# A fused transformer layer and expert feed-forward: attention in steps of two head pairs, value projections of 512 columns

## The chip, the cores and the metric

The kernel runs on one core of a Trainium2 chip. Its engines are TensorE (PE, matmuls; its weight loads are shown as PEld), VectorE (DVE), ScalarE (ACT), GpSimd (POOL) and SyncE (SP, which issues the DMAs). The metric is the device time of one execution in microseconds; the median of the runs counts, and lower is better. Of the kernel before there are 3 timed runs.

## The reference

All in float32, for x of 8 x 256 x 256 (batch, tokens, features):

```python
def attention(x, ctx, mask, wq, wk, wv, wo, bo):        # 16 heads of 64
    q, k, v = (heads of x @ wq), (heads of ctx @ wk), (heads of ctx @ wv)
    sim = einsum('bhid,bhjd->bhij', q, k) * 64 ** -0.5
    sim = where(mask[:, None, None, :], neg, sim)
    out = einsum('bhij,bhjd->bhid', softmax(sim), v)
    return out as (b, n, 1024) @ wo + bo

h = layernorm(x)                                        # no gain, no bias
h = layernorm(h + attention(h, h, mask, sa_...), ln1)
h = layernorm(h + attention(h, ctx_1024, mask, ca_...), ln2)
h = layernorm(h + gelu(h @ fc1_w + fc1_b) @ fc2_w + fc2_b, ln3)
x = x + h
xf = layernorm(x)
y = geglu(xf, w1s, w2s, w3s) + geglu(xf, W1[e], W2[e], W3[e])   # e = argmax(xf @ Wg) of 8
return x + y
```

## The kernel before

The instructions of each engine are written out by hand, one list per engine, and the engines meet through counting semaphores. The program has three parts: the attention (self layer, then cross layer, up to some 770 us), a dense stage of 8 steps (fc1, fc2) and a stage of expert steps. The change touches the first part and the passage to the second.

Every float32 product is made of three fast ones (`product`, L49 to L54): each operand is split into a high part (`_hi`, rounded by a copy) and a low part (`_lo`, what is left), and low x high, high x low and high x high are summed in PSUM. So each tensor that PE multiplies costs a copy on ACT (or DVE) and a subtraction on DVE (or POOL).

A **turn** u is one batch element in one layer: 16 turns, 0 to 7 of the self layer, 8 to 15 of the cross layer. A turn has 8 **pairs** of heads; pairs i are counted through, 128 in all (`NPAIR`). For a pair:
- `project_qk(i)`: q and k of both heads into one bank `ps_pj`; ACT copies it (`hi_of_bank`), DVE subtracts (`lo_of_bank`, L1515).
- `scores(i)` (L960): 12 matmuls of 64 rows, two heads side by side, into `ps_s[0]` and `ps_s[1]`. They wait for qk's low part (`pj_lo`) and for the masked maxima of the pair before (`max_ready`).
- `masked_max(i, h)` (L1533): DVE adds the mask, writes `scores` to SBUF and takes the row extreme `nb`.
- `exps(i, h)` (L1294): ACT, `probs` and their sums; `invert_sums` (L1543, DVE); `normalise` (L669, POOL).
- `transpose_probs(i, h)` (L970): 4 PE transposes per head into `ps_t[h]`; ACT copies (`hi_of_probs`, L1301), DVE subtracts (`lo_of_probs`, L1547).
- `attend(i)` (L983): 8 matmuls into `ps_pv`, of which there is one; high and low part of the values stand side by side, so that the product comes in two halves. ACT copies the lower half (`cross_of_pair`, L1305), DVE adds it to the upper (`join_pair`, L1555, two adds), ACT and POOL split the result (`hi_of_pair` L1310, `lo_of_pair` L688). The next `attend` waits for the join.
- `output(i)`: 6 matmuls into `ps_aux`, two pairs at a time.

Besides, every second pair `project_v(g)` makes the values of the next two pairs (group g, 12 matmuls of 256 columns; L1282, L1513), and once per turn the next turn's rows are transposed (`xq`), in the cross layer its context too (`xc`; L1519). DVE adds the residual once per turn (L1563) and takes row statistics: of the output of the turn before (`output_stats`) and, in the self layer, of the next input (`input_stats`; L1568, L1571). POOL norms rows (L674 to L678), applies gain and bias (L701, L702) and the attention's bias (L710). The weights of a layer come in as 512-column pieces: DVE copies the high part (L1499), POOL subtracts (L719), at pairs given by `PIECES_IN`.

The order around the change is one loop over i on each engine. In iteration i PE issues scores(i+1), transposes of i, project_qk(i+2), on even i output of two pairs, on some the values or rows, attend(i-1). DVE does the maxima of i+1, join of i-2, then the low parts, and after them rows, weight pieces and statistics. The names of the banks are shared out by `bank_events`, which lists everything that goes through the two `ps_pj` in order.

Of the kernel before, what the change touches and what calls it, by code (L numbers as in the profile page):

```python
# [75 lines left out]

def bank_events():

    order = [("xq", 0), ("qk", 0), ("qk", 1), ("v", 0)]
    for i in range(NPAIR):  # L80
        u, p = i // PAIRS, i % PAIRS
        if i + 2 < NPAIR:
            order.append(("qk", i + 2))
        if p == CTX_AT and u + 1 < NTURN and layer_of(u + 1):
            order.append(("xc", u + 1))
        if p == ROWS_AT and u + 1 < NTURN:
            order.append(("xq", u + 1))
        if p % 2 == 1 and i + 1 < NPAIR:
            order.append(("v", (i + 1) // 2))
        if i == FIRST_ROWS_AT:  # L90
# [1787 lines left out]
```

## Time and profile before

| | us |
|---|---|
| runs: median (lowest to highest) | 1227.9 (1227.55 to 1228.11) |
| the profiled execution | 1228.37 |
| its span, first to last instruction | 1226.6 |
| PE busy in it | 1211.9 |
| DVE busy | 981.8 |
| ACT busy | 874.9 |
| POOL busy | 681.2 |

The span is what the trace covers; the execution's own time has 1.8 us around it. Busy time counts the work of an engine, not its waits. A matmul's record shows how long it takes from start to end, 0.28 us, though the next starts 0.12 us later; what matmuls cost is therefore read from start to start. The same holds for ACT and DVE, whose instructions overlap a little.

### The profile page before, as it was taken

Reading aid. Unit: us, or ns where it says so; the run is one execution under the profiler, and the core shown is the slowest. Engines: PE = TensorE matmul, PEld = TensorE weight load, DVE = VectorE, ACT = ScalarE, POOL = GpSimd, SP = SyncE. Lnnn points to the kernel's source line nnn. Section 1 sums busy time; section 2 is a strip of 40 time slices with the busy share of each in tenths; the row PEclk is TensorE's granted clock in tenths of the full one; section 3 lists DMA queues with packets and bytes.
Section 4 is the critical chain, followed back from the end, with each engine's and each line's share of the span. In section 5 each row is a group of like instructions: output and inputs, shape, how many; then the busy total and the mean of one; then the engine's idle time right before and its main releaser. Section 6 shows DMA issues by size and latency. Waiting matters only on the chain.

```text
span 1226.6 us, 31369 instructions
## 1 busy us (share of the span) xinstructions
PE 1211.9 (99%) x10444; PEld 1163.3 (95%) x10444; DVE 981.8 (80%) x2674; ACT 874.9 (71%) x2259; POOL 681.2 (56%) x1089
## 2 busy tenths in 40 slices
PE   8999999999999999999999999999999999999998
PEld 6899999999999999999999999999999999999998
DVE  6888888988989988888888889854554888888854
ACT  6988888878887888888888788543433677767732
POOL 5766656656678855555565477887624033432231
PEclk9999999999999999999999999999999999999999
DMA  6060000000000002200000010111013677788722
GB/s 198 4 248 19 18 3 19 10 11 19 7 22 27 2 27 110 91 27 28 2 28 28 2 36 12 35 41 47 1 64 122 190 262 252 251 257 277 236 69 78
DMA packets 72207, 97.46 MB, mean 79 GB/s; under 512 B 5488, under 2 KB 52464, under 8 KB 72048
## 3 DMA queue, kind: packets, MB, share of 16 engines
q1 hardware_dynamic: 70512, 91.25, 22.9%
q0 software_dynamic: 1536, 4.20, 1.1%
q8 instruction: 86, 1.41, 0.5%
q14 instruction: 73, 0.60, 0.2%
HBM read 81.01 MB, written 14.42 MB: 78 GB/s over the span
## 4 chain that ended last, share of the span: by engine, by line
PE 84%; DVE 6%; ACT 5%; issue 3%; DMA 1%; SPq 0%; DVEq 0%; ACTq 0%
PE ps_pj L52 9%; PE ps_pj L54 9%; PE ps_pj L53 9%; PE ps_t L970 8%; PE ps_s L960 8%; PE ps_pv L983 8%; PE ps_aux L54 4%; PE ps_aux L52 4%; PE ps_aux L53 4%; ACT probs L1294 4%; PE ps_s L54 4%; PE ps_s L53 4%; PE ps_s L52 4%; PE ps_pv L54 2%; PE ps_pv L52 2%
## 5 line engine op out<-in xcount | busy, mean ns | idle before, releaser
L669 POOL TENSOR_SCALAR probs<-probs,inv 128x256 f32<-128x256 f32 x512 | 235.7, 479 | 220.9 <-DVE inv L1543 220.2
L1294 ACT ACTIVATE probs<-scores,nb 128x256 f32<-128x256 f32 x512 | 253.7, 497 | 16.5 <-DVE nb L1533 16.0
L1533 DVE CUSTOM_DVE_ANT_0 scores<-ps_s,maskf 128x256 f32<-128x256 f32 x512 | 186.7, 420 | 54.1 <-PE ps_s L960 51.7
L1301 ACT ACTIVATE probs_t_hi<-ps_t 128x512 fp32r<-128x512 f32 x256 | 150.7, 589 | 99.7 <-PE ps_t L970 99.6
L1547 DVE TENSOR_TENSOR probs_t_lo<-ps_t,probs_t_hi 128x512 fp32r<-128x512 f32 x256 | 172.8, 675 | 0.4
L970 PE MATMUL ps_t<-ident,probs 128*128 128x128 f32 x1024 | 139.9, 279 | 0.6 <-POOL probs L669 0.6
L52 PE MATMUL ps_pj<-xq_hi,wq_lo 128*128 128x256 f32 x448 | 138.1, 308 | 0.1
L983 PE MATMUL ps_pv<-probs_t_lo,v_stack 128*128 128x256 f32 x512 | 130.3, 287 | 1.1 <-issue 1.0
L983 PE MATMUL ps_pv<-probs_t_hi,v_stack 128*128 128x256 f32 x512 | 127.7, 282 | 0.0
L970 PEld LDWEIGHTS ps_t<-ident,probs 128*128 128x128 f32 x1024 | 109.7, 141 | 17.8 <-POOL probs L669 0.9
L54 PE MATMUL ps_pj<-xq_hi,wq_hi 128*128 128x256 f32 x448 | 126.2, 282 | 0.0
L53 PE MATMUL ps_pj<-xq_lo,wq_hi 128*128 128x256 f32 x448 | 126.2, 282 | 0.0
L688 POOL TENSOR_TENSOR heads_t_lo<-joined,heads_t_hi 128x256 fp32r<-128x256 f32 x128 | 94.6, 739 | 31.1 <-ACT heads_t_hi L1310 30.7
L1555 DVE TENSOR_TENSOR joined<-ps_pv,cross 64x256 f32<-64x256 f32 x256 | 106.1, 415 | 3.0 <-ACT cross L1305 1.2
L1515 DVE TENSOR_TENSOR qk_lo<-ps_pj,qk_hi 128x512 fp32r<-128x512 f32 x128 | 88.5, 691 | 14.1 <-ACT qk_hi L1285 2.9
L983 PEld LDWEIGHTS ps_pv<-probs_t_lo,v_stack 128*128 128x128 f32 x512 | 97.9, 191 | 1.7 <-issue 1.7
L816 POOL TENSOR_TENSOR wq_lo<-raw,wq_hi 128x512 fp32r<-128x512 f32 x14 | 18.1, 1294 | 145.7 <-ACT wq_hi L1408 145.7
L983 PEld LDWEIGHTS ps_pv<-probs_t_hi,v_stack 128*128 128x128 f32 x512 | 98.0, 191 | 0.0
L1385 ACT ACTIVATE gelu<-ps_pj 128x512 f32<-128x512 f32 x78 | 46.5, 596 | 72.2 <-PE ps_pj L54 71.0
L1294 ACT ACTIVATION_READ_ACCUMULATOR probs<-scores,nb 128x1 f32 x512 | 95.6, 187 | 0.0
L1394 ACT ACTIVATE gt_hi<-ps_s 128x512 fp32r<-128x512 f32 x64 | 38.3, 599 | 75.7 <-DVE ps_s L1603 75.7
L960 PE MATMUL ps_s<-qk_hi,qk_lo 64*128 64x256 f32 x512 | 85.5, 331 | 6.7 <-DVE qk_lo L1515 6.0
(275 smaller groups left out, 4439.5 us busy)
## 6 DMA issues: line engine op xcount, KB each, us to landing
raw<-in_L_ffn_W SPq DMA_DIRECT2D x90, 512.0 KB, 4.9
slot_rows<-hin SPq DMA_DIRECT2D x3, 768.0 KB, 6.1
rows<-in_x SPq DMA_DIRECT2D x8, 256.0 KB, 2.7
after_self<-rows SPq DMA_DIRECT2D x8, 256.0 KB, 2.1
rows<-after_self SPq DMA_DIRECT2D x8, 256.0 KB, 2.7
cin<-in_ctx SPq DMA_DIRECT2D x8, 256.0 KB, 3.0
after_cross<-rows SPq DMA_DIRECT2D x8, 256.0 KB, 2.7
stage<-in_L_xattn_fc_w SPq DMA_DIRECT2D x2, 1024.0 KB, 9.0
```

The source lines that it names most:

```text
L52: pe.matmul(out, wl, mh, start=start, stop=False, skip_group_check=True)
L53: pe.matmul(out, wh, ml, start=False, stop=False, skip_group_check=True)
L54: return pe.matmul(out, wh, mh, start=False, stop=stop, skip_group_check=True)
L669: last = pool.tensor_scalar(PR[:, h, t, :], PR[:, h, t, :], inv[:, h, t:t + 1], 1.0, ALU.mult, ALU.mult)
L960: last = pe.matmul(ps_s[h][:, t * S:(t + 1) * S], q[a][half, t * P:(t + 1) * P], k[b][half, :], start=t == 0 and n == 0, stop=t == ST - 1 ...
L970: last = pe.transpose(ps_t[h][:, j * S + t * P:j * S + (t + 1) * P], PR[:, h, t, j * P:(j + 1) * P], ident[:, :])
L983: last = pe.matmul(ps_pv[:, h * S:(h + 1) * S], v, x[:, i % 2, h, j, :], start=h == 0 and j == 0 and x is PT[1], stop=j == ST - 1 and x is ...
L1294: last = act.activation(PR[:, h, t, :], SM[:, h, t, :], ACT.Exp, bias=nb[:, h, t:t + 1], scale=-1.0, accum_out=sums[:, h, t:t + 1])
L1301: act.activation(flat(PT[0][:, i % 2, h, :, :]), ps_t[h][:, :], ACT.Copy).then_inc(t_hi, 1)
L1533: last = dve.tensor_tensor_reduce(SM[:, h, t, :], ps_s[h][:, t * S:(t + 1) * S], maskf[:, i // PAIRS % 2, :], -SCALE, -LOWEST, ALU.add, AL ...
L1547: dve.tensor_tensor(flat(PT[1][:, i % 2, h, :, :]), ps_t[h][:, :], flat(PT[0][:, i % 2, h, :, :]).bitcast(F32), ALU.subtract).then_inc(t_l ...
L1555: last = dve.tensor_tensor(joined[h * DH:(h + 1) * DH, i % 2, :], ps_pv[0:DH, h * S:(h + 1) * S], cross[:, h, :], ALU.add)
```

## The change

The attention runs in **steps of two pairs**: step k works on i = 2k, 63 steps (`TURNS_OF_TWO`), four to a turn.
- PE in step k: scores of pairs i+2 and i+3, project_qk(i+4), attend(i), values, transposes of i+1 and i+2, project_qk(i+5), output of two pairs, rows or context, attend(i+1).
- Scores of even pairs go to `ps_s`, of odd pairs to `ps_t`, and the transposes of a pair go to the other two banks (`scores_bank`, `turned_bank`). Scores now wait for the low parts of the probabilities transposed through that bank (`t_lo`), transposes for the maxima that empty theirs.
- The masked maxima write into `probs` itself, of which there are now three, and `nb`, `sums`, `inv` are doubled.
- DVE starts a step with the join of pair i-1, ahead of the maxima of i+2 and i+3.
- From turn 1 on, a value group is one of the two 128-row tiles of the keys for four pairs (`project_v`: 6 matmuls of 512 columns in place of 12 of 256), and `VS` is two blocks of four pairs.
- Weight pieces, statistics, norms and rows are put to steps in place of pairs. The load of the shared w3 waits for the last attend. Two of the dense stage's first products change places with banks.

```diff
+AHEAD = [("v", 1), ("q", 2), ("k", 2), ("q", 3)]
+STARTS = (0, 26, 58)
+PIECES_IN = [{0: [("k", 3), ("v", 2), ("o", 0)], 1: [("v", 3), ("o", 1)], 2: [("o", 2)], 3: [("o", 3)]},
+             {0: [("q", 0), ("k", 0)], 1: [("q", 1), ("v", 0)], 2: [("k", 1), ("v", 1), ("q", 2)], 3: [("k", 2), ("v", 2)],
+              4: [("v", 3), ("q", 3)], 5: [("k", 3), ("o", 0)], 6: [("o", 1)], 7: [("o", 2)], 8: [("o", 3)]},
+             {0: [("q", 0), ("k", 0)], 1: [("v", 0), ("q", 1)], 2: [("k", 1), ("q", 2)], 3: [("v", 1), ("q", 3)],
+              4: [("o", 0)], 5: [("o", 1)], 6: [("o", 2)], 7: [("o", 3)], 8: [("k", 2), ("v", 2), ("k", 3), ("v", 3)]}]
...
             def project_v(g):
...
+                else:
+                    t, half = g % 2, k // 2
                     for c in range(KC):
+                        last = product(pe, bank[:, :], tuple(x[:, c, t * P:(t + 1) * P] for x in kv_of(u)),
+                                       tuple(w[:, c * INNER + half * 512:c * INNER + (half + 1) * 512] for w in W["v"]),
+                                       c == 0, c == KC - 1)
...
             def scores(i):
                 pe.wait_ge(pj_lo, EVENT[("qk", i)] + 1)
-                wait(pe, max_ready, 2 * i)
+                if i == 2:
+                    pe.wait_ge(max_ready, 2)
+                elif i > 2:
+                    pe.wait_ge(t_lo, 2 * (i - 2))
...
             def transpose_probs(i, h):
                 pe.wait_ge(norm_ready, 2 * i + h + 1)
-                wait(pe, t_lo, 2 * (i - 1) + h + 1)
+                if i == NPAIR - 1:
+                    pe.wait_ge(t_lo, 2 * (i - 2) + h + 1)
+                else:
+                    pe.wait_ge(max_ready, 2 * (i + 1) + h + 1)
```

PE's list (in part; the old loop over i is taken out):

```diff
+            for k in range(TURNS_OF_TWO):
+                i = 2 * k
+                scores(i + 2)
+                scores(i + 3)
+                if i + 4 < NPAIR:
+                    project_qk(i + 4)
+                attend(i)
+                for g in values_in(k):
+                    project_v(g)
...
+                for n in (i + 1, i + 2):
+                    transpose_probs(n, 0)
+                    transpose_probs(n, 1)
+                if i + 5 < NPAIR:
+                    project_qk(i + 5)
+                if k >= 1:
+                    output(i - 2)
+                    output(i - 1)
+                if turn_rows(k) is not None:
+                    what, u = turn_rows(k)
+                    (transpose_ctx if what == "xc" else transpose_rows)(u)
+                attend(i + 1)
```

ACT's list of a step:

```diff
+                if k >= 1:
+                    cross_of_pair(i - 1)
+                exps(i + 2, 0)
+                exps(i + 2, 1)
+                if i + 4 < NPAIR:
+                    hi_of_bank(("qk", i + 4))
+                if k >= 1:
+                    hi_of_pair(i - 1)
+                cross_of_pair(i)
+                exps(i + 3, 0)
+                for g in values_in(k):
+                    hi_of_bank(("v", g))
...
+                hi_of_probs(i + 1, 0)
+                hi_of_probs(i + 1, 1)
+                hi_of_pair(i)
+                hi_of_probs(i + 2, 0)
+                hi_of_probs(i + 2, 1)
+                exps(i + 3, 1)
+                if i + 5 < NPAIR:
+                    hi_of_bank(("qk", i + 5))
+                if turn_rows(k) is not None:
+                    hi_of_bank(turn_rows(k))
```

DVE's list of a step:

```diff
+                if k >= 1:
+                    join_pair(i - 1)
+                masked_max(i + 2, 0)
+                masked_max(i + 2, 1)
+                invert_sums(i + 2, 0)
+                masked_max(i + 3, 0)
+                invert_sums(i + 2, 1)
+                masked_max(i + 3, 1)
+                if i + 4 < NPAIR:
+                    lo_of_bank(("qk", i + 4))
+                join_pair(i)
+                invert_sums(i + 3, 0)
+                if p == 1 and u >= 1:
+                    residual_sum(u - 1)
+                for g in values_in(k):
+                    lo_of_bank(("v", g))
...
+                lo_of_probs(i + 1, 0)
+                lo_of_probs(i + 1, 1)
+                lo_of_probs(i + 2, 0)
+                lo_of_probs(i + 2, 1)
+                invert_sums(i + 3, 1)
+                if i + 5 < NPAIR:
+                    lo_of_bank(("qk", i + 5))
+                if turn_rows(k) is not None:
+                    lo_of_bank(turn_rows(k))
+                if k < TURNS_OF_TWO - 1:
+                    late_hi_pieces(k)
...
+                if p == 1 and u >= 1:
                     output_stats(u - 1)
-                if p == 1 and u + 1 < B:
+                if p == 0 and u + 1 < B:
                     input_stats(u + 1)
```

The built programs show the order that results. On ACT, in the cross layer, two pairs before (L1301 copies transposed probabilities, L1294 is the exponentials, L1285 qk, L1282 values, L1310 a joined pair, L1305 the crossing half):

```order
L1294 ACTIVATE probs,sums<-scores,nb 128x256 x4
L1285 ACTIVATE qk_hi<-ps_pj 128x512
L1301 ACTIVATE probs_t_hi<-ps_t 128x512
L1310 ACTIVATE heads_t_hi<-joined 128x256
L1305 ACTIVATE cross<-ps_pv 64x512
L1301 ACTIVATE probs_t_hi<-ps_t 128x512
L1294 ACTIVATE probs,sums<-scores,nb 128x256 x4
L1285 ACTIVATE qk_hi<-ps_pj 128x512
L1301 ACTIVATE probs_t_hi<-ps_t 128x512
L1282 ACTIVATE v_stack<-ps_pj 128x8x64
L1310 ACTIVATE heads_t_hi<-joined 128x256
L1305 ACTIVATE cross<-ps_pv 64x512
```

and one step of two pairs in the change (L1359, L1352, L1342, L1339, L1368, L1363 in the same meaning):

```order
L1363 ACTIVATE cross<-ps_pv 64x512
L1352 ACTIVATE probs_68,sums<-probs_68,nb 128x256 x4
L1342 ACTIVATE qk_hi<-ps_pj 128x512
L1368 ACTIVATE heads_t_hi<-joined 128x256
L1363 ACTIVATE cross<-ps_pv 64x512
L1352 ACTIVATE probs_69,sums<-probs_69,nb 128x256 x2
L1339 ACTIVATE v_stack_61<-ps_pj 128x8x64
L1359 ACTIVATE probs_t_hi<-ps_s 128x512 x2
L1368 ACTIVATE heads_t_hi<-joined 128x256
L1359 ACTIVATE probs_t_hi<-ps_t 128x512 x2
L1352 ACTIVATE probs_69,sums<-probs_69,nb 128x256 x2
L1342 ACTIVATE qk_hi<-ps_pj 128x512
```

The exponentials of four heads now stand in three places (two heads, one, one), the first of them right behind a crossing copy, and the copy of the second qk is last in the step.

On DVE, one pair before, from its last masked maximum (L1533) to the next pair's first (L1555 join, L1543 inverted sums, L1547 and L1515 low parts of probabilities and qk):

```order
L1533 ISA scores,nb<-ps_s,maskf 128x256
L1533 ISA nb 128x1
L1555 TENSOR_TENSOR joined<-ps_pv,cross 64x256 x2
L1543 RECIPROCAL inv<-sums 128x2
L1547 TENSOR_TENSOR probs_t_lo<-ps_t,probs_t_hi 128x512
L1543 RECIPROCAL inv<-sums 128x2
L1515 TENSOR_TENSOR qk_lo<-ps_pj,qk_hi 128x512
L1547 TENSOR_TENSOR probs_t_lo<-ps_t,probs_t_hi 128x512
L1533 ISA scores,nb<-ps_s,maskf 128x256
```

and the second half of a step in the change, up to the next step's first maximum (L1589, L1633, L1621, L1587, L1625, L1610 in the same meaning; L1593 is the low part of the context):

```order
L1589 TENSOR_TENSOR qk_lo<-ps_pj,qk_hi 128x512
L1633 TENSOR_TENSOR joined<-ps_pv,cross 64x256 x2
L1621 RECIPROCAL inv<-sums 128x2
L1587 TENSOR_TENSOR v_stack_61<-ps_pj,v_stack_61 128x8x64
L1625 TENSOR_TENSOR probs_t_lo<-ps_s,probs_t_hi 128x512 x2
L1625 TENSOR_TENSOR probs_t_lo<-ps_t,probs_t_hi 128x512 x2
L1621 RECIPROCAL inv<-sums 128x2
L1589 TENSOR_TENSOR qk_lo<-ps_pj,qk_hi 128x512
L1593 TENSOR_TENSOR xc_lo<-ps_pj,xc_hi 128x512
L1633 TENSOR_TENSOR joined<-ps_pv,cross 64x256 x2
L1610 ISA probs_69,nb<-ps_s,maskf 128x256
```

The join has moved from behind the maxima to ahead of them, and the low parts of the second qk and of the context, which stood behind the probabilities' low parts, now stand just ahead of that join.

On PE, the switch from scores (L960) to transposes (L970) to projections before:

```order
L960 MATMUL ps_s<-qk_lo,qk_hi 128x256 x2
L960 MATMUL ps_s<-qk_hi 128x256 x2
L970 MATMUL ps_t<-ident,probs 128x128 x8
L52 MATMUL ps_pj<-xq_hi,wq_lo 128x256
L53 MATMUL ps_pj<-xq_lo,wq_hi 128x256
```

and scores to projections (L999 is the scores) in the change:

```order
L999 MATMUL ps_s<-qk_lo,qk_hi 128x256 x2
L999 MATMUL ps_s<-qk_hi 128x256 x2
L999 MATMUL ps_t<-qk_hi,qk_lo 128x256 x2
L999 MATMUL ps_t<-qk_lo,qk_hi 128x256 x2
L999 MATMUL ps_t<-qk_hi 128x256 x2
L999 MATMUL ps_t<-qk_hi,qk_lo 128x256 x2
L999 MATMUL ps_t<-qk_lo,qk_hi 128x256 x2
L999 MATMUL ps_t<-qk_hi 128x256 x2
L52 MATMUL ps_pj<-xq_hi,wq_lo 128x256
L53 MATMUL ps_pj<-xq_lo,wq_hi 128x256
L54 MATMUL ps_pj<-xq_hi,wq_hi 128x256
```

Scores of an even pair and an odd pair stand together, and projections follow them.

## Rows read from the trace of the kernel before

**Rows 1.** The page, span and part 1: busy time and share of the span.

```profile
span 1226.6 us, 31369 instructions
...
PE 1211.9 (99%) x10444; PEld 1163.3 (95%) x10444; DVE 981.8 (80%) x2674; ACT 874.9 (71%) x2259; POOL 681.2 (56%) x1089
```

**Rows 2.** Windows view, one self turn: us; busy PE, PEld, DVE, ACT, POOL; clock; DMA.

```profile
302.78:349.43 46.65, 46.55 (x422) 44.33 (x420) 40.76 (x135) 38.06 (x109) 29.03 (x55) 1.00 0.06 19
```

**Rows 3.** Timeline, PE, one pair: start, us, what (x how many).

```profile
650.28 0.28 PE L983 MATMUL ps_pv<-probs_t_hi,v_stack 128*128 128x256 f32 x1
...
650.72 0.28 PE L960 MATMUL ps_s<-qk_lo,qk_hi 64*128 64x256 f32 x2
...
651.19 0.28 PE L960 MATMUL ps_s<-qk_hi 64*128 64x256 f32 x2
651.40 1.09 PE L970 MATMUL ps_t<-ident,probs 128*128 128x128 f32 x8
...
652.45 0.28 PE L53 MATMUL ps_pj<-xq_lo,wq_hi 128*128 128x256 f32 x1
```

**Rows 4.** Timeline, PE, start-up, where projections follow scores.

```profile
16.72 0.31 PE L960 MATMUL ps_s<-qk_hi 64*128 64x256 f32 x2
...
17.18 0.28 PE L53 MATMUL ps_pj<-xq_lo,wq_hi 128*128 128x256 f32 x1
...
18.49 1.04 PE L970 MATMUL ps_t<-ident,probs 128*128 128x128 f32 x8
...
19.49 0.28 PE L53 MATMUL ps_pj<-xq_lo,wq_hi 128*128 128x256 f32 x1
```

**Rows 5.** Timeline, PE, 512 moving columns, in the routed stage.

```profile
980.22 0.40 PE L53 MATMUL ps_pj<-wk_lo,xq_hi 128*128 128x512 f32 x1
980.45 0.39 PE L54 MATMUL ps_pj<-wk_hi,xq_hi 128*128 128x512 f32 x1
```

**Rows 6.** Timeline, ACT, one pair.

```profile
646.83 0.50 ACT L1294 ACTIVATE probs<-scores,nb 128x256 f32<-128x256 f32 x1
...
648.81 0.57 ACT L1285 ACTIVATE qk_hi<-ps_pj 128x512 fp32r<-128x512 f32 x1
649.28 0.58 ACT L1301 ACTIVATE probs_t_hi<-ps_t 128x512 fp32r<-128x512 f32 x1
...
650.24 0.41 ACT L1310 ACTIVATE heads_t_hi<-joined 128x256 fp32r<-128x256 f32 x1
650.67 0.60 ACT L1305 ACTIVATE cross<-ps_pv 64x512 f32<-64x512 f32 x1
```

**Rows 7.** Timeline, DVE, the same pair.

```profile
647.04 0.42 DVE L1533 CUSTOM_DVE_ANT_0 scores<-ps_s,maskf 128x256 f32<-128x256 f32 x1
...
647.39 0.85 DVE L1555 TENSOR_TENSOR joined<-ps_pv,cross 64x256 f32<-64x256 f32 x2
...
649.41 0.69 DVE L1515 TENSOR_TENSOR qk_lo<-ps_pj,qk_hi 128x512 fp32r<-128x512 f32 x1
650.02 0.68 DVE L1547 TENSOR_TENSOR probs_t_lo<-ps_t,probs_t_hi 128x512 fp32r<-128x512 f32 x1
...
651.22 0.74 DVE L1568 BATCH_NORM_STATS2 part<-rows 128x6 f32<-128x256 f32 x2
...
652.27 0.42 DVE L1533 CUSTOM_DVE_ANT_0 scores<-ps_s,maskf 128x256 f32<-128x256 f32 x1
```

**Rows 8.** Timeline, PE, scores of pairs 10, 50, 74 and 122.

```profile
68.78 0.39 PE L960 MATMUL ps_s<-qk_hi,qk_lo 64*128 64x256 f32 x2
...
302.87 0.39 PE L960 MATMUL ps_s<-qk_hi,qk_lo 64*128 64x256 f32 x2
...
445.17 0.39 PE L960 MATMUL ps_s<-qk_hi,qk_lo 64*128 64x256 f32 x2
...
726.61 0.39 PE L960 MATMUL ps_s<-qk_hi,qk_lo 64*128 64x256 f32 x2
```

**Rows 9.** Line view, L1499: 128x512 copies of weight pieces, min/median/max ns.

```profile
L1499 DVE CAST wk_hi<-stage x8: 412/475/1503, 356.0 to 779.6; 128x512 fp32r<-128x512 f32 x8
```

More of the change, by code:

```diff
@@ L74, in layer_of, with turn_rows @@
     return u // B
-def bank_events():
[L79 to L90, printed above, removed]
+def turn_rows(k):
+    u = k // STEPS_PER_TURN + 1
+    if u < NTURN and k % STEPS_PER_TURN == 0 and layer_of(u):
+        return ("xc", u)
+    if u < NTURN and k % STEPS_PER_TURN == 1:
+        return ("xq", u)
+    return None
@@ L91, in bank_events, with values_in @@
+def values_in(k):
+    if k < 3:
+        return ((1,), (2,), (3, 4))[k]
+    return (k + 2,) if 2 * k + 4 < NPAIR else ()
+def bank_events():
+    order = [("xq", 0), ("qk", 0), ("qk", 1), ("v", 0), ("qk", 2), ("qk", 3)]
+    for k in range(TURNS_OF_TWO):
+        if 2 * k + 4 < NPAIR:
+            order.append(("qk", 2 * k + 4))
+        order += [("v", g) for g in values_in(k)]
+        if k == TURNS_OF_TWO - 1:
             order.append(("h", 0))
+        if 2 * k + 5 < NPAIR:
+            order.append(("qk", 2 * k + 5))
+        if turn_rows(k) is not None:
+            order.append(turn_rows(k))
@@ L128, in set_of @@
+PIECES_AT = {start + at: pieces for start, plan in zip(STARTS, PIECES_IN) for at, pieces in plan.items()}
 def set_of(i):
-    return sum(i >= base for base in BASES[1:])
+    return sum(i >= start for start in STARTS[1:])
 LATE = [(0, kind, q) for kind, q in AHEAD] + [(set_of(j), kind, q) for j in sorted(PIECES_AT) for kind, q in PIECES_AT[j]]
@@ L863, in _ @@
+            split_late(TURNS_OF_TWO - 1)
             lo_of_pair(NPAIR - 2)
-            split_late(NPAIR)
+            split_late(TURNS_OF_TWO)
             lo_of_pair(NPAIR - 1)
-            for i in range(NPAIR + 1, NPAIR + 4):
-                split_late(i)
+            split_late(TURNS_OF_TWO + 1)
+            split_late(TURNS_OF_TWO + 2)
             bias_rows(0)
@@ new lines, in _ @@
+            scores(1)
+            project_qk(2)
+            transpose_probs(0, 0)
+            transpose_probs(0, 1)
+            project_qk(3)
+            for k in range(TURNS_OF_TWO):
+                i = 2 * k
+                scores(i + 2)
[5 more added lines that the diff above has]
+                    project_v(g)
+                if k == TURNS_OF_TWO - 1:
+                    transpose_first(0)
+                for n in (i + 1, i + 2):
[10 more added lines that the diff above has]
+                attend(i + 1)
@@ L1215, in _ @@
+            up_dense(0, 0)
+            attend(NPAIR - 2)
+            up_dense(0, 1)
+            transpose_probs(NPAIR - 1, 0)
+            transpose_probs(NPAIR - 1, 1)
+            output(NPAIR - 4)
+            output(NPAIR - 3)
+            attend(NPAIR - 1)
+            transpose_step(1)
+            up_dense(0, 2)
+            up_dense(0, 3)
+            output(NPAIR - 2)
+            output(NPAIR - 1)
             down(0, range(FC))
@@ L1280, in hi_of_bank @@
                 if kind == "v":
-                    wait(act, pv_done, 2 * (k - 1))
-                    last = act.activation(v_part(k, 0), v_rows(bank), ACT.Copy)
+                    wait(act, pv_done, 4 * (k // 2 - 1))
+                    last = act.activation(v_part(k, 0), v_rows(bank, k), ACT.Copy)
                 elif kind == "qk":
```

316 lines of the change are left out of this document (146 added, 170 removed), and 6 rows, old and new, of the table PIECES_IN.

## The prediction

> **What bounds the kernel now.** I read first the page's part 1: TensorE (PE) is busy 1211.9 of 1226.6 us, VectorE (DVE) 80%, ScalarE (ACT) 71% [rows 1]. Then one turn of the attention, 46.65 us long: PE 46.55 busy, DVE 40.76, ACT 38.06, POOL 29.03, clock 1.00 [rows 2]. So PE sets the pace, and DVE has 5.9 us of slack in a turn of eight pairs. The change touches the attention alone; the rest is read as fixed. The reader is to see two more things. A turn of the self layer takes (302.87 - 68.78)/5 = 46.8 us, the three turns in which the second layer's weight pieces come in take 142.3 together, and the six up to pair 122 take 281.4, 46.9 each [rows 8]. And PE's own stream has gaps that are no waits: matmuls of 256 columns follow each other every 0.12 us, but where the 64-row scores begin two intervals take 0.44 in place of 0.24 (+0.20), from scores to transposes 0.21 (+0.09), and from the first transpose to the second projection matmul behind the eight it is 1.05 [rows 3], against 1.00 where no scores stood just before (+0.05) [rows 4].
>
> **The change on PE.** For two pairs the old order pays 2 x (0.20 + 0.09 + 0.05) = 0.68 us of these switches. The new one issues the scores of two pairs together, puts projections behind them, and transposes both pairs together behind other matmuls. That is one entry (0.20) and one way out to projections, which the start-up shows as 0.46 for 0.24 (+0.22) [rows 4], and nothing ahead of the transposes. Scores of one pair straight behind those of another occur nowhere in the trace: between 0 and 0.20; I take 0, for within a pair the scores follow each other without a gap. So 0.42, a saving of 0.26 in each of 63 steps, 16.4 us. Value projections: from turn 1 on a group is 6 matmuls of 512 columns in place of 12 of 256, in 60 groups, 360 fewer. 512 columns take 0.23 [rows 5] against 2 x 0.12, so 12 x 0.12 - 6 x 0.23 = 0.06 less a group, 3.6 us in all. PE alone would then need 20.0 us less. A pair takes it (46.55 - 0.44)/8 = 5.76 us now (the turn's four transposes of rows taken off at 0.11), so a step of two pairs 11.52 - 0.26 - 0.06 = 11.20 us.
>
> The Trainium skill (TensorE: Matmul & The Clock Gate, Back-to-back issue gap) gives N/2.4 + 2.5 ns for a gap, 109 and 216 ns: by the page a group would gain 12 x 109 - 6 x 216 = 12 ns, 0.7 us in all. The rows show 120 and 230, and decide.
>
> **The change on DVE and ACT.** Their work stays the same, but the new order ties them into a loop. I walk through one step k, i = 2k, from the start of the join of pair i-1 (J), with start-to-start times of [rows 6, 7]:
> - DVE: the join is two adds, 0.85; head 0 of pair i+2 then takes two masked maxima at 0.35 and 0.07 until the last one ends. With a hand-over of 0.03 (ACT's copy of qk ends at 648.81 + 0.57 = 649.38, its low part starts at 649.41) ACT starts its exponentials at J + 1.65. Until then ACT had only the crossing copy of pair i-1 to do, which the join itself needed.
> - ACT from there has an unbroken list up to the copy of qk(i+5): four heads' exponentials at 0.99 (646.83 to 648.81 is two heads), 3.96; qk(i+4) 0.47; values 0.48; four copies of transposed probabilities 1.92; two of joined pairs 0.86; one crossing copy, between 0.43 (as the joined pair's) and 0.60 (its duration), I take 0.50, what other copies of 512 columns take; the copy of qk(i+5) 0.57 and hand-over 0.03. Sum 8.79, so J + 10.44. PE is not waited for in it: PE's scores begin 0.74 before J, and 1.6 of scores, 1.6 of projection, 1.0, 1.4 of values and 1.7 of transposes end at J + 6.6; the copies of the last two heads start at 7.9 and 8.4.
> - DVE then takes the low part of qk(i+5), 0.61: J + 11.05. Behind it stands the join of pair i+1.
>
> So the loop takes 11.05 us, just under PE's 11.20. That is the bare step. Whatever DVE does between that low part and the next join is added whole, since ACT has nothing meanwhile: the low part of the next turn's rows or context 0.60; statistics 1.05 (651.22 to 652.27) [rows 7]; a weight piece some 0.45 (0.475 [rows 9] less a little overlap). Before, these stood in DVE's slack ahead of the maxima, where ACT had transposed probabilities to copy. The residual sum (0.6, an add of 128x512) stays free: DVE idles about as long at the wait for the last exponentials behind it.
>
> Can PE hide the excess? Little. Its next step needs qk(i+5) split for its second scores, which leaves some 0.15 us of room; past that PE stands. POOL is busy 29.0 us in a turn [rows 2], 7.3 per step; it is off this loop except where a step bunches its work (a rival, below). SP: context, rows and weights are still issued a step or more ahead. The one load moved behind the last attention is w3s, needed a dense step later: no cost; if late, its copies on ACT would hold the second dense step.
>
> **The sum.** A self turn: 4 x 11.05 + 0.60 rows + 1.05 input + 1.05 output statistics + 0.1 (PE's 11.20 in the step where the lag is gone) = 47.0. A cross turn: 44.2 + 1.2 + 1.05 + 0.1 = 46.55.
> - Turn 0: two copies of first weight pieces (0.48 each) enter ACT's list in step 0: +1.0.
> - Turns 1 to 5: 5 x 47.0 = 235.0 against 234.1: +0.9.
> - Turns 6 to 8: 47.0 + 4 pieces (1.8); turn 7, without input statistics, 44.2 + 1.2 + 1.05 + 9 pieces (4.05) = 50.5; turn 8 46.55 + 3 pieces (1.35). Together 147.2 against 142.3: +4.9.
> - Turns 9 to 14: 6 x 46.55 + 4 pieces = 281.1 against 281.4: -0.3.
> - Last turn and the passage to the dense stage: both orders wait there; between -4 and +2, I take -1.
>
> That is +5.5 us. The profiled execution took 1228.4 (its span 1226.6), 0.5 above the median of the runs, 1227.9. So 1233.9 for an execution like the profiled one, 1233.4 as the median.
>
> **Rivals.**
> - *PE stays the bound*: the loop is cut somewhere (extras fall into DVE's idle time, ACT starts before the join is done). Then switches and projections count in full: 1227.9 - 20.0 = 1207.9. For it: PE is 99% busy, nothing else is near it. Against: DVE would need 40.8 of 45.2 us and never be waited for. Chance 0.14. The Trainium skill (Perfetto Trace Analysis, Identifying the Most-Contended Engine) says to optimize the engine of the highest occupancy first; by that rule PE's savings pay and this rival wins. The walk above is where I part from it.
> - *The loop is shorter by 0.15 a step* (join and maxima overlap more, a cheaper crossing copy): 0.15 x 63 = 9.5 less, 1224. Chance 0.20.
> - *Slower still, through POOL*: in a turn's third step POOL norms the output rows between the pairs it normalises. It decides once that step's work passes 11.2, 4 us above its mean of 7.3, and normalised probabilities come later than PE's transposes want them. At 0.6 us in each of 14 turns, 8.4: 1242. Chance 0.11.
> - *The change does not do what it says*: the built order shows 360 fewer matmul rows and the moves quoted above. No chance given.
>
> **Numbers.** Forecast 0.55, by itself 1227 to 1240 (0.1 us a step is 6 us in all). A difference under 0.2%, 2.5 us, is what a measurement of this kernel can't tell from none. Faster by more: 0.14 of PE's bound, 0.11 of the shorter loop: 0.25. Same: 0.09 of the shorter loop, 0.07 of the forecast: 0.16. Slower: 0.59. The range, 1214 to 1243, leaves out PE's bound and a little above.
>
> **What would show it.** Right: PE waits for qk_lo (L1589) at the scores of odd pairs, most in the steps behind statistics; ACT's largest wait is at the exponentials, for DVE's nb, 1.0 us or more a step; turns of 47.0 and 46.6; PE busy falls by some 20 us while the span grows; no gap from scores to scores; values every 0.23. Wrong: turns of 45.2 to 45.7 with PE above 98%; a bare step well off 11.1; ACT waiting mostly for PE's transposes, as before; statistics that do not lengthen their step.

## The result, and the profile of the changed kernel

The changed kernel takes 1257.79 us (median of 4 runs, 1255.87 to 1259.34) against 1228.01 (4 runs, 1227.55 to 1228.42): a ratio of 1.024, 95% interval 1.0227 to 1.0253. I had said 1233.4, 1214 to 1243. The sign was right, the size was not: 5.5 us more were forecast and 29.8 came. The profiled execution took 1258.6 us, its span is 1256.9, 30.3 above the span of before [rows 1].

The page of the changed kernel, with the chain of waits (its part 4):

```profile
span 1256.9 us, 30952 instructions
...
PE 1221.2 (97%) x10084; PEld 1150.6 (92%) x10084; DVE 983.4 (78%) x2674; ACT 879.0 (70%) x2259; POOL 685.6 (55%) x1089
...
PE 59%; DVE 14%; ACT 14%; issue 9%; POOL 1%; DVEq 1%; DMA 1%; SPq 0%; ACTq 0%; POOLq 0%
```

The work of DVE, ACT and POOL is what it was, but DVE and ACT now hold 28% of the chain. Before, it was 11%:

```profile
PE 84%; DVE 6%; ACT 5%; issue 3%; DMA 1%; SPq 0%; DVEq 0%; ACTq 0%
```

The waits over the whole span (engine, tile and line, what it waited for; us, times, longest) name the place:

```profile
ACT probs L1352 <- DVE nb L1610: 145.1, 65, 4.2
...
DVE inv L1621 <- ACT probs L1352: 64.3, 114, 1.1
...
PEld ps_t L999 <- DVE qk_lo L1589: 17.9, 33, 1.7
```

ACT stands 2.2 us in each step until DVE's first maxima are there, and PE's scores of odd pairs wait for the low part of qk: the two signs that the prediction named. The windows view (us; busy PE, PEld, DVE, ACT, POOL; clock; DMA) of the four steps of a self turn, cut at the attention products of pairs 40, 42, 44, 46 and 48:

```profile
271.24:282.57 11.33, 11.33 (x101) 10.66 (x100) 9.66 (x32) 8.63 (x25) 6.80 (x12) 1.00 0.01 2
282.57:294.75 12.18, 12.18 (x104) 11.14 (x103) 10.83 (x34) 9.95 (x28) 7.28 (x15) 1.00 0.00 0
294.75:307.53 12.78, 11.92 (x100) 10.65 (x99) 10.74 (x39) 10.34 (x30) 9.47 (x17) 1.00 0.01 3
307.53:318.82 11.29, 11.29 (x101) 10.66 (x99) 9.51 (x31) 9.44 (x28) 5.54 (x11) 1.00 0.15 48
```

The same four steps took 11.68, 11.95, 11.50 and 11.51 before, 46.64 in all, and take 47.58 now. The two bare steps are shorter than before, by 0.35 and 0.22; the two behind statistics are longer, by 0.23 and 1.28.

One bare step of the loop, from the join of pair 43 to that of pair 45, in ACT's and DVE's timelines (start, us). DVE first:

```profile
293.71 0.81 DVE L1633 TENSOR_TENSOR joined<-ps_pv,cross 64x256 f32<-64x256 f32 x2
294.56 0.42 DVE L1610 CUSTOM_DVE_ANT_0 probs<-ps_s,maskf 128x256 f32<-128x256 f32 x1
...
304.35 0.69 DVE L1589 TENSOR_TENSOR qk_lo<-ps_pj,qk_hi 128x512 fp32r<-128x512 f32 x1
304.96 0.84 DVE L1633 TENSOR_TENSOR joined<-ps_pv,cross 64x256 f32<-64x256 f32 x2
```

```profile
295.37 0.51 ACT L1352 ACTIVATE probs<-probs,nb 128x256 f32<-128x256 f32 x1 [2.73 <-DVE nb L1610]
...
297.26 0.19 ACT L1352 ACTIVATION_READ_ACCUMULATOR probs<-probs,nb 128x1 f32 x1
297.48 0.60 ACT L1342 ACTIVATE qk_hi<-ps_pj 128x512 fp32r<-128x512 f32 x1
...
298.90 0.50 ACT L1352 ACTIVATE probs<-probs,nb 128x256 f32<-128x256 f32 x1
...
300.00 0.60 ACT L1339 ACTIVATE v_stack<-ps_pj 128x512 fp32r<-128x512 f32 x1
...
303.60 0.23 ACT L1352 ACTIVATION_READ_ACCUMULATOR probs<-probs,nb 128x1 f32 x1
303.69 0.62 ACT L1342 ACTIVATE qk_hi<-ps_pj 128x512 fp32r<-128x512 f32 x1
```

So the loop is there, link by link: join to first exponential 295.37 - 293.71 = 1.66 (forecast 1.65); ACT's list 304.35 - 295.37 = 8.98 (8.79); low part 0.61 (0.61); together 11.25 where I had 11.05.

**Places that the prediction did not walk.** In the third step of turn 0 (group 4 shares its bank with qk of pair 8) and in the last step, PE stands over 2 us. Its timeline at the two:

```profile
54.32 0.28 PE L54 MATMUL ps_pj<-wv_hi,xq_hi 128*128 128x256 f32 x1
56.96 0.77 PE L52 MATMUL ps_pj<-wv_hi,xq_lo 128*128 128x512 f32 x1 [2.36 <-DVE qk_lo L1589]
...
793.69 0.28 PE L54 MATMUL ps_aux<-wo_hi,heads_t_hi 128*128 128x256 f32 x1
796.15 0.39 PE L52 MATMUL ps_aux<-wo_hi,heads_t_lo 128*128 128x256 f32 x1 [2.17 <-POOL heads_t_lo L697]
```

and the windows around them, where the last but two columns are the granted clock:

```profile
54.00:56.00 2.00, 0.60 (x6) 0.40 (x4) 1.59 (x9) 1.95 (x7) 1.54 (x4) 1.00 0.00 0
56.00:58.00 2.00, 1.04 (x3) 0.88 (x4) 1.76 (x7) 1.90 (x6) 1.16 (x3) 0.67 0.01 4
58.00:60.00 2.00, 2.00 (x7) 1.51 (x6) 0.65 (x1) 0.10 (x1) 0.79 (x2) 0.50 0.00 0
...
794.00:796.00 2.00, 0.00 (x0) 0.00 (x0) 0.78 (x2) 0.25 (x1) 1.92 (x3) 1.00 0.00 0
796.00:798.00 2.00, 1.85 (x13) 1.85 (x14) 0.43 (x1) 0.00 (x0) 2.00 (x3) 0.84 0.71 217
798.00:800.00 2.00, 2.00 (x11) 2.00 (x11) 0.80 (x2) 1.41 (x3) 1.47 (x2) 0.50 0.68 196
```

Around the end of each wait the clock falls from 2.4 to 1.2 GHz for some 3 us, and the 512-column matmuls of group 4 follow each other every 0.43 us.

A third place lies in the last turn: PE's attention product waits 1.53 us for a join that stands on DVE behind two weight pieces and the statistics, and here too the clock falls (rows of DVE and PE, then the window).

```profile
777.07 0.54 DVE L1573 CAST wv_hi<-stage 128x512 fp32r<-128x512 f32 x1
777.87 0.74 DVE L1646 BATCH_NORM_STATS2 part<-rows 128x6 f32<-128x256 f32 x2
778.80 0.81 DVE L1633 TENSOR_TENSOR joined<-ps_pv,cross 64x256 f32<-64x256 f32 x2
779.72 0.36 PE L1025 MATMUL ps_pv<-probs_t_lo,v_stack 128*128 128x256 f32 x1 [1.53 <-issue]
...
780.00:782.00 2.00, 2.00 (x13) 2.00 (x12) 1.28 (x9) 1.54 (x7) 0.00 (x0) 0.58 0.00 0
```

With the one at 26 us (last section) the profiled execution has four such stretches of some 3.4 us, and the kernel before has none in its attention. An estimate from these windows: at half the clock they cost at most 4 x 1.7 = 6.8 us of the 30.3.

Where the 30.3 us of span went, by the starts of the attention products, beside what I had forecast for each stretch (for the first, no term at all):

| stretch | before | after | more | forecast |
|---|---|---|---|---|
| start to attention product 0 | 25.7 | 27.9 | 2.1 | 0 |
| turn 0 | 47.8 | 52.3 | 4.5 | 1.0 |
| turns 1 to 5 | 234.1 | 238.7 | 4.6 | 0.9 |
| turns 6 to 8 | 142.3 | 151.1 | 8.8 | 4.9 |
| turns 9 to 14 | 281.4 | 285.6 | 4.2 | -0.3 |
| last turn and all behind it | 495.3 | 501.3 | 6.0 | -1 |

### The profile page after: what moved, and what is told of

It is laid out like the page before. It is cut to its first block, busy times and chain, and to the rows that moved or that the text cites. A ratio compares the mean times of both kernels' runs of the same rounds, so it can differ in the third digit from the quotient of the medians.

```text
span 1256.9 us, 30952 instructions
## 1 busy us (share of the span) xinstructions
PE 1221.2 (97%) x10084; PEld 1150.6 (92%) x10084; DVE 983.4 (78%) x2674; ACT 879.0 (70%) x2259; POOL 685.6 (55%) x1089
## 4 chain that ended last, share of the span: by engine, by line
PE 59%; DVE 14%; ACT 14%; issue 9%; POOL 1%; DVEq 1%; DMA 1%; SPq 0%; ACTq 0%; POOLq 0%
PE ps_pj L52 7%; PE ps_pj L53 6%; PE ps_pj L54 6%; ACT probs_t_hi L1359 6%; ACT probs L1352 5%; DVE probs L1610 5%; PE ps_pv L1025 4%; PE ps_s L52 4%; PE ps_s L54 4%; PE ps_s L53 4%; DVE qk_lo L1589 3%; PE ps_aux L52 3%; PE ps_aux L54 3%; PE ps_aux L53 3%; PE ps_t L999 2%
## 5 line engine op out<-in xcount | busy, mean ns | idle before, releaser
L678 POOL TENSOR_SCALAR probs<-probs,inv 128x256 f32<-128x256 f32 x512 | 242.0, 485 | 261.6 <-DVE inv L1621 260.0
L1352 ACT ACTIVATE probs<-probs,nb 128x256 f32<-128x256 f32 x512 | 256.2, 507 | 145.1 <-DVE nb L1610 145.1
L1610 DVE CUSTOM_DVE_ANT_0 probs<-ps_t,maskf 128x256 f32<-128x256 f32 x256 | 98.4, 422 | 24.3 <-issue 15.8
L1633 DVE TENSOR_TENSOR joined<-ps_pv,cross 64x256 f32<-64x256 f32 x256 | 105.1, 411 | 7.3 <-ACT cross L1363 5.5
L1352 ACT ACTIVATION_READ_ACCUMULATOR probs<-probs,nb 128x1 f32 x512 | 101.0, 197 | 0.0
L52 PEld LDWEIGHTS ps_pj<-xq_hi,wq_lo 128*128 128x128 f32 x448 | 85.1, 190 | 13.0 <-DVE qk_lo L1589 0.9
L1459 ACT ACTIVATE gelu<-ps_pj 128x512 f32<-128x512 f32 x78 | 46.4, 595 | 72.2 <-PE ps_pj L54 70.9
L1621 DVE RECIPROCAL inv<-sums 128x2 f32<-128x2 f32 x256 | 42.1, 164 | 68.0 <-ACT probs L1352 64.3
L1589 DVE TENSOR_TENSOR qk_lo<-ps_pj,qk_hi 128x512 fp32r<-128x512 f32 x128 | 88.1, 688 | 8.7 <-ACT qk_hi L1342 3.0
L1610 DVE CUSTOM_DVE_ANT_0 probs<-ps_s,maskf 128x256 f32<-128x256 f32 x256 | 93.3, 421 | 1.9
L53 PEld LDWEIGHTS ps_pj<-xq_lo,wq_hi 128*128 128x128 f32 x448 | 85.6, 191 | 0.0
L54 PEld LDWEIGHTS ps_pj<-xq_hi,wq_hi 128*128 128x128 f32 x448 | 85.5, 191 | 0.0
```

The costliest lines, as they stand in the source:

```text
L52: pe.matmul(out, wl, mh, start=start, stop=False, skip_group_check=True)
L53: pe.matmul(out, wh, ml, start=False, stop=False, skip_group_check=True)
L54: return pe.matmul(out, wh, mh, start=False, stop=stop, skip_group_check=True)
L678: last = pool.tensor_scalar(x, x, inv[:, i % 2, h, t:t + 1], 1.0, ALU.mult, ALU.mult)
L1352: last = act.activation(x, x, ACT.Exp, bias=nb[:, i % 2, h, t:t + 1], scale=-1.0, accum_out=sums[:, i % 2, h, t:t + 1])
L1459: act.activation(G[:, f % 2, :], ps_u[f % 2][:, :], ACT.Gelu).then_inc(g_ready, 1)
```

## Experiments

Runs 1 to 4, 5 to 8 and 9 to 12 were timed in three sets, each beside the kernel before, whose medians were 1228.1, 1227.9 and 1228.4 us. A median is of 4 executions where nothing else is said.

**1. The join behind the maxima.** One part of the change undone:

```diff
-                if k >= 1:
-                    join_pair(i - 1)
                 masked_max(i + 2, 0)
                 masked_max(i + 2, 1)
+                if k >= 1:
+                    join_pair(i - 1)
```

> VectorE takes the two masked maxima pairs of pair i+2 ahead of the join of pair i-1; nothing else moves. Theory 1 (a loop through VectorE and ScalarE sets the step; the join of 0.85 us stands in it ahead of the maxima): the exponentials start some 0.75 us earlier in each step, the bare step of 11.28 us falls to what PE needs (11.20) and the steps with extras lose the whole 0.75. Self turn 47.6 -> 45.3 to 46.1, total 1224 to 1236, 1230 expected. Theory 2 (PE's own waits for the second bank of transposes and the late second scores set the step, the join is beside it): within 2 us of 1257.8. Theory 3 (the join is then late for the next attention product, PE waits for it instead): above 1257.8.

Measured: 1257.41 us (1256.09 to 1258.07), as the changed kernel. DVE's and PE's timelines show why:

```profile
292.99 0.84 DVE L1633 TENSOR_TENSOR joined<-ps_pv,cross 64x256 f32<-64x256 f32 x2
```

```profile
293.09 0.28 PE L54 MATMUL ps_pj<-xq_hi,wk_hi 128*128 128x256 f32 x1
293.94 0.35 PE L1025 MATMUL ps_pv<-probs_t_lo,v_stack 128*128 128x256 f32 x1 [0.57 <-issue]
```

PE's attention product of pair i writes the bank that the join of pair i-1 reads; with the join behind the maxima of both heads it stands until 293.83, and PE waits 0.57 us here and in every step (3.9 us in eight steps). Bare steps are 11.80, 0.5 longer than in the changed kernel. The number is the one of theory 2, "within 2 us of 1257.8", but it is a sum: turns 9 to 14 take 290.9 us against 285.6, while turn 0 takes 50.1 against 52.3 and the last stretch 497.8 against 501.3. Theory 3's wait is in the trace and outweighs theory 1's gain in the bare step. This run alone can't tell whether the loop was cut; run 6 does.

**2. Statistics moved** from the end of a step to behind the first two maxima of the next.

```diff
                 masked_max(i + 2, 1)
+                if p == 2 and u >= 1:
+                    output_stats(u - 1)
+                if p == 1 and u + 1 < B:
+                    input_stats(u + 1)
                 invert_sums(i + 2, 0)
...
-                if p == 1 and u >= 1:
-                    output_stats(u - 1)
-                if p == 0 and u + 1 < B:
-                    input_stats(u + 1)
```

> The statistics of input and output rows (1.05 us each, 7 + 15 of them inside the steps) move from behind the low part of qk(i+5) to behind the first masked maxima of the next step, where VectorE stands idle for 0.7 us. Theory 1 (work behind the low part of qk(i+5) is added whole to its step, work behind the maxima is not): 22 x 1.05 = 23 us less, 1235 (1232 to 1240), self turn 45.5. Theory 2 (the step is long for another reason, statistics only fill the wait): 1257 to 1259.

Measured: 1237.54 us (1236.87 to 1238.32), 20.3 less than the changed kernel, 0.92 for each of the 22 passes, in the range of theory 1. No work was taken away. The same four steps:

```profile
261.83:273.15 11.32, 11.32 (x101) 10.66 (x100) 9.70 (x32) 9.49 (x28) 6.80 (x12) 1.00 0.01 2
273.15:284.75 11.60, 11.60 (x104) 11.02 (x103) 11.14 (x38) 9.69 (x29) 7.28 (x15) 1.00 0.00 0
284.75:296.32 11.57, 11.44 (x101) 10.66 (x99) 10.40 (x37) 9.75 (x28) 9.48 (x17) 1.00 0.01 3
296.32:307.63 11.31, 11.31 (x101) 10.66 (x100) 9.50 (x31) 9.47 (x28) 5.54 (x11) 1.00 0.16 48
```

The steps with statistics fell from 12.18 and 12.78 to 11.60 and 11.57; the bare ones stay. What stands between the low part of qk(i+5) and the next maxima is added to the step, as the prediction had it.

**3. Values of 256 columns.** `if u == 0:` in `project_v` and `if g < GROUPS` in the two helpers for the layout hold for all turns.

> Undoes one part of the change: all value groups are 12 matmuls of 256 columns again, over the two blocks of four pairs; the order of the engines stays. Theory 1 (PE is not the bound): its 60 x 0.06 = 3.6 us are mostly hidden, 1257.8 to 1259.5. Theory 2 (the 512-column groups or their blocks of four pairs cause the loss, as PE's waits at value banks suggest): below 1250. Theory 3 (PE is the bound all the same): 1261.4.

Measured: 1256.98 us (1256.29 to 1258.96). 512 columns give nothing and cost nothing here.

**4. A dose in the loop.**

```diff
                 dve.wait_ge(pj_hi, m + 1)
+                if twice:
+                    for t in range(ST):
+                        dve.bn_stats(part[:, 2, t, :], QK[0][:, k % 2, t, :].bitcast(F32))
```

> Two statistics passes over qk_hi (0.335 us each, 0.67 together; their result is not used) stand ahead of the low part of qk(i+5) on VectorE in 62 steps. Theory 1: 62 x 0.67 = 41.5 us more, 1299; 1293 at least, if some steps had room. Theory 2 (VectorE has slack, at 78% busy): less than 10 us more.

Measured: 1297.45 us (1295.61 to 1299.16), 39.7 more, 0.64 in each of 62 steps. The dose in DVE's timeline, and a bare step of 11.93 in which DVE is idle for 1.8 us:

```profile
316.38 0.75 DVE L1588 BATCH_NORM_STATS2 part<-qk_hi 128x6 f32<-128x256 f32 x2
317.05 0.67 DVE L1592 TENSOR_TENSOR qk_lo<-ps_pj,qk_hi 128x512 fp32r<-128x512 f32 x1
...
320.22:332.15 11.93, 11.44 (x101) 10.66 (x100) 10.11 (x33) 9.48 (x28) 5.17 (x10) 1.00 0.14 45
```

DVE, 78% busy over the span, passes on 95% of what is put into it at this place.

**5. The join between the two heads' maxima**, on top of run 2.

> As the run with the statistics moved (1237.5 us), and the join of pair i-1 stands between the masked maxima of the two heads of pair i+2. Theory 1 (two prices of the join's place: ahead of both heads ScalarE's exponentials start late; behind both, PE's next attention product starts late): head 0's exponentials start 0.7 us earlier, head 1's some 0.2, and PE's attention product has its join 0.6 us before it asks for it. Steps of 11.3 to 11.75 us fall to 11.2 to 11.4, turns of 45.8 and 46.4 to 45.4 and 45.7: 1228 (1224 to 1233). Theory 2 (ScalarE's list after the join does not matter any more, another wait sets these steps): 1236 to 1239.

Measured: 1238.62 us (1235.36 to 1239.23), no gain, the expectation missed. In eight steps ACT waits for DVE's nb 16 times, 16.2 us in all; in run 2 it is 8 times and 15.9 us. The wait was split, not shortened. Turns 1 to 5 even take 233.6 us against 229.8 in run 2, and turn 0 takes 49.5 against 51.2; what makes the turns longer was not followed up.

**6. Maxima first, and the join's price on PE paid:** on top of runs 1 and 2, PE projects the values ahead of attention product i, and ACT and DVE take their parts of pair i behind the values.

```diff
-                attend(i)
                 for g in values_in(k):
                     project_v(g)
+                attend(i)
```

> As the run with the statistics moved, and the join of pair i-1 stands behind both heads' masked maxima, while PE projects the values ahead of attention product i (1.4 us more time for the join); ScalarE and VectorE take the copy and the join of pair i behind the values accordingly. Theory 1: the loop is 10.6 us, PE's 11.2 sets every step, turns of 45.3: 1224 (1219 to 1230). Theory 2 (maxima first is a loss in itself, as the run with them first could be read): 1237 or more.

Measured: 1232.87 us (1231.92 to 1235.41), 4.7 less than run 2. The four steps:

```profile
263.21:274.44 11.23, 11.23 (x100) 10.69 (x98) 9.77 (x32) 9.55 (x28) 6.19 (x11) 1.00 0.01 2
274.44:286.70 12.26, 12.05 (x103) 11.11 (x102) 11.66 (x40) 10.32 (x29) 7.32 (x15) 1.00 0.01 1
286.70:298.49 11.79, 11.48 (x99) 10.68 (x98) 10.40 (x37) 9.60 (x28) 10.76 (x19) 1.00 0.01 2
298.49:309.64 11.15, 11.15 (x99) 10.63 (x98) 9.33 (x30) 9.22 (x28) 4.96 (x11) 1.00 0.14 48
```

Bare steps are PE's now, 11.15 (forecast for PE: 11.20), so the loop is cut. But this run lies above its range: the two steps with statistics are longer than in run 2. DVE takes the statistics ahead of the maxima of pair i+3, and ACT waits for these; in the second step, with residual sum, rows and input statistics, DVE is busy 11.66 of 12.26 us. The extras found a second bound; run 10 tests it. In plain self turns this order even loses: turns 1 to 5 take 232.8 us against 229.8 in run 2. Its gain lies elsewhere: turns 6 to 8 take 144.6 against 148.1, turn 0 48.9 against 51.2, the last stretch 496.4 against 499.2.

**7. The two ends mended**, on top of run 2: group 4 behind the transposes on PE, ACT and DVE; POOL's low part of pair 125 between the two weight pieces of the last step. POOL's part of the edit:

```diff
-                    split_late(k - 1)
+                    for n, (kind, q) in enumerate(PIECES_AT[k - 1]):
+                        if n == 1:
+                            lo_of_pair(NPAIR - 3)
+                        late_low(2, kind, q)
```

> As the run with the statistics moved, and two places at the ends: in the third step of turn 0 the second value group stands behind the transposes on all engines (its bank waits for the low part of qk that VectorE takes behind all maxima), and in the last step GpSimd takes the low part of pair 125 between two weight pieces instead of behind them and the rows. If those two waits (2.4 and 2.2 us on PE) and the halved TensorE clock that follows each are what turn 0 and the end lost: 3 to 4 us at the start, 2 to 3 at the end, 1231 (1229 to 1235), and the granted clock stays 1.00 in both places. If they are hidden by others: 1236 to 1238.

Measured: 1234.11 us (1233.05 to 1234.6), 3.4 less than run 2 and in the range. The windows at the first place, with the clock at 1.00 throughout:

```profile
56.00:58.00 2.00, 2.00 (x10) 1.35 (x10) 1.77 (x5) 1.98 (x7) 1.16 (x3) 1.00 0.02 4
58.00:60.00 2.00, 1.80 (x15) 1.74 (x15) 2.00 (x5) 2.00 (x5) 1.04 (x2) 1.00 0.00 0
```

That step fell from 16.57 us (run 2) to 13.89, and the stretch from attention product 120 to 127 from 40.83 to 38.10, 5.4 together in the profiled executions. In the same two executions 0.9 us is lost again up to attention product 0, where this one shows a granted clock of 0.57 from 26 to 30 us and run 2 shows 1.00, and 0.9 behind product 127, for which no cause was found. At the second place only the wait was mended: in run 2 PE waits there for 2.47 us and the granted clock is 1.00 all the same.

**8. Values of 256 columns on run 2.**

> As the run with the statistics moved, and value groups of 256 columns. Theory 1 (steps of 11.3 are loop and PE nearly even now): some of the 3.6 us of PE show, 1238 to 1241. If values of 256 columns cost nothing here either: 1237 to 1238.

Measured: 1237.68 us (1236.04 to 1238.98), no difference from run 2's 1237.54: with steps of 11.3 and more the loop still hides the 0.06 us a group.

**9. Weight pieces on ACT**, on top of runs 6 and 7, and the input statistics in the turn's first step.

```diff
                 if k >= 1:
                     cross_of_pair(i - 1)
+                    late_hi_act(k - 1)
                 exps(i + 2, 0)
...
-                if k < TURNS_OF_TWO - 1:
-                    late_hi_pieces(k)
```

> The run with maxima first and values ahead (1232.9), with three more edits: both mended ends (third step of turn 0, GpSimd's order in the last step), the copies of late weight pieces taken by ScalarE at the start of the next step, where it stands idle for 1.5 us, instead of by VectorE ahead of the maxima, and the input statistics in the turn's first step instead of the second. Theory 1 (a step is as long as the loop or VectorE's own list, which is full in steps with extras): ends -3.4, turns 6 to 8 and 14 fall from 48.0, 49.9, 46.8, 47.5 to some 46.5 each (-6), input statistics 0 to -0.3 in each self turn: 1223 (1219 to 1227), faster than the kernel before. If the copies only change their place and ScalarE's list becomes the loop: 1229 to 1232.

Measured: 1225.45 us (10 runs, 1224.46 to 1227.21), ratio to before 0.9977 (0.9967 to 0.9987). Turns 6, 8 and 14 take 46.8, 46.4 and 46.4, as their neighbours, and turn 7 47.5. One part of the expectation missed: turns 1 to 5 take 234.2 us against 232.8 in run 6, where the moved input statistics were to give 0 to 0.3 each.

**10. Statistics behind all four maxima**, on top of run 9: the same lines, behind `masked_max(i + 3, 1)`.

> As the run with the pieces on ScalarE, and the statistics stand behind all four masked maxima of a step, ahead of the low part of qk(i+4). Where they stand in that run they hold the maxima of pair i+3 and so ScalarE. Theory 1 (what counts is that ScalarE is not held): 0.3 us less in each of 22 steps, 1217 (1213 to 1223). Theory 2 (VectorE itself is full in these steps: 10.1 us of work and events and 1.05 on top are PE's 11.2): within 2 us of the run it starts from.

Measured: 1217.9 us (1216.06 to 1218.17), ratio 0.9912 (0.9896 to 0.9929): 10.5 us faster than the kernel before, 39.9 faster than the change as it stood. 7.6 less than run 9, or 0.34 for each of 22 passes. Its page and chain:

```profile
span 1214.3 us, 30952 instructions
...
PE 1199.9 (99%) x10084; PEld 1145.5 (94%) x10084; DVE 971.6 (80%) x2650; ACT 895.1 (74%) x2283; POOL 680.6 (56%) x1089
...
PE 90%; DVE 3%; issue 2%; ACT 2%; POOL 1%; DMA 1%; SPq 0%; DVEq 0%; ACTq 0%; POOLq 0%
```

PE holds 90% of the chain (84% before), so it is the bound again in most steps. Cross turns take 45.9 us (46.9 before).

**11. Run 9 with values of 256 columns.**

> As the run with the pieces on ScalarE, with value groups of 256 columns. In the earlier pairs 512 columns gave nothing, since PE was not the bound. If PE now sets about half of the steps, 60 x 0.06 us come out by half: 1.5 to 2.5 us more than that run; if in no step: 0 to 0.5.

Measured: 1227.76 us (10 runs, 1226.81 to 1228.78), 2.3 more than run 9, 0.04 of the 0.06 a group: the value part pays as soon as PE sets part of the steps.

**12. Join ahead of the maxima as in the change, statistics, ends and pieces as mended** (run 7 with the pieces on ACT).

> The run with the mended ends (1234.1, join ahead of the maxima as in the change, statistics moved), with the copies of late weight pieces taken by ScalarE where it waits for the masked maxima. Turns 6, 7, 8 and 14 (47.8, 51.8, 48.4, 48.3) should come near the plain turns of 45.8 and 46.4: 8 to 10 us less, 1225 (1222 to 1229). If a wait for the pieces themselves (GpSimd's low parts) is what makes turn 7 long: 1230 to 1234.

Measured: 1220.55 us (1219.85 to 1221.41), ratio 0.9932 (0.9916 to 0.9949), better than its range. Turns 6, 7, 8 and 14 in run 7 went from 47.8, 51.8, 48.4 and 48.3 to 45.9, 47.3, 46.5 and 46.4, 10.3 us for 20 pieces, 0.51 each; the pieces of the last turn give some 2 more, which I had left out. So even the change's own join order beats the kernel before, once nothing else stands in its loop. In turns 1 to 5 it is the best of all, 229.7 us against 231.0 in run 10, though its bare steps stay at 11.3; run 10 gains in turn 0, the cross turns and the last turn. The join ahead of the maxima with the statistics behind all of them was not run.

## Why the prediction was right in kind and wrong in size

- **PE's savings: right.** A bare step of PE's own is 11.15 us (run 6) against 11.50 before; 0.26 + 0.06 = 0.32 were forecast, 0.35 came. Scores behind scores have no gap where nothing is waited for, as I took it: in the changed kernel's PE timeline the 0.12 goes on across the change of banks.

```profile
479.11 0.28 PE L999 MATMUL ps_s<-qk_hi 64*128 64x256 f32 x2
479.23 0.28 PE L999 MATMUL ps_t<-qk_hi,qk_lo 64*128 64x256 f32 x2
479.35 0.28 PE L999 MATMUL ps_t<-qk_lo,qk_hi 64*128 64x256 f32 x2
```

- **The values, 3.6 us not binding: right** (runs 3 and 8: nothing; run 11: 2.3). In the changed kernel a group's 6 matmuls take 1.39 us (295.71 to 297.11), 0.05 less than 12 x 0.12. The formula of the Trainium skill (TensorE: Matmul & The Clock Gate, Back-to-back issue gap) gives an estimate of 0.7 us in all; the 2.3 measured speak for the rows.
- **The loop: right as a mechanism, 0.2 short.** Runs 2 and 4 move and dose it. The term that failed is "four heads' exponentials at 0.99, 3.96": they take 4.19. Where a copy follows the exponentials the hand-over is 0.21 to 0.22 (297.26 to 297.48) in two of three places, and I had taken the 0.09 that stands between two exponentials [rows 6]. The rest of the list comes to 0.04 less than forecast. A bare step is 11.25 to 11.33, not 11.05 to 11.15. Times 63 that is some 12 us, and I had put "0.1 us a step is 6 us in all" down myself.
- **Extras added whole: right.** Statistics 0.92 by run 2 (1.05 forecast), pieces 0.51 by run 12 (0.45 forecast). A self turn is 47.6 (47.0), a cross turn 47.3 (46.55). Turns 1 to 14 were forecast 5.5 us longer than before and are 17.6 longer; these 0.6 to 0.8 a turn make up most of the 12.1 between.
- **Turn 0, "+1.0": wrong.** I costed two copies on ACT and did not follow group 4 through the two banks: it is the step's second group, its bank waits for the low part of qk(8), and that stands on DVE behind all maxima. 2.4 us of wait and the clock behind it. Besides, group 1 (1.4 us of PE), which before stands ahead of attention product 0, now stands behind it. Run 7 takes 2.7 of it back.
- **The start, no term: wrong.** Attention product 0 comes at 27.9 in place of 25.7. In run 2, with the same lists up to there and the clock at 1.00, it comes at 26.7; so some 1.2 us go with the clock that falls at 26 us, and some 1.0 with the new order.
- **Last turn, "-1": wrong.** I wrote that both orders wait there. The new wait is on POOL: the low part of pair 125 stands behind two weight pieces (1.46 each) and the rows' two operations (1.29 each). I had walked POOL's queue for the third step of a turn only. And the pieces and statistics, which I added to the steps of every other turn, stand ahead of a join here too (1.53 us of PE's wait at 779.72).
- **The range was too narrow for this.** I bounded single costs and gave no width to what a list of costs leaves out, and all that it left out lay on one side. Of the signs, waits for qk_lo, ACT's wait for nb, scores without a gap and values every 0.23 came; turns were 0.6 to 0.8 above. PE's busy time did not fall by 20 but rose by 9.3: a matmul's record lasts 0.28 us while the next starts after 0.12, so short waits count as busy, and the stretches at 1.2 GHz lengthen it. In run 10 it is 12.0 below before.
- **The rivals.** *The loop is shorter by 0.15* was false: it is 0.2 longer. *PE stays the bound* was false for the change and nearly true for run 10, 1217.9 against the 1207.9 worked out: a bare step of PE's own is shorter by what was forecast, and half of the 20 us were had. The rule of the Trainium skill (Perfetto Trace Analysis, Identifying the Most-Contended Engine), to take the most-contended engine first, would have given 1207.9 here. For TensorE the page judges by the rate of useful work and the share of weight loads, not by the share of matmuls; before, the weight loads were busy 95% of the span, more than DVE, ACT and POOL, and the matmuls 99%. The trace of the change goes against the rule, since PE at 97% (weight loads 92%) waits on engines at 78% and 70%. *Through POOL* was false in the turns as far as the trace shows: POOL has 9.5 of 12.8 us in its fullest step, PE's transposes wait there 0.4 us for its probabilities (8.3 us in 20 waits over the whole span), and ACT's list has no gap behind that. It was true in the last turn.

## What to carry to other kernels

When an order ties two engines into a loop, walk the loop once, then ask of every operation of both engines on which side of it the operation stands: the same 23 us of statistics cost 20 us more at one place than at another, on an engine that looks one fifth idle. A saving on the busiest engine is had only down to the length of the loop: bare steps of 11.50 us fell to 11.3 with the loop in place and to 11.15 with it cut. Measure the loop with a dose, as in run 4. And walk the first and the last step of each queue: a steady step says nothing about them, and here the start, turn 0 and the last turn lost 12.6 of the 30.3 us.
